# A four-part graph network on one core: batches from high destinations first, ten compare rows on ScalarE, the encoder's chunks shifted by two, and the first unit of a GRU step made in the sweep before it

## The reference

```
x = layernorm(x + gcn3(x))        # three convolutions h = segment_sum((h @ W)[src] * norm, dst) + b, then @ Wl + bl
x = layernorm(x + sage2(x))       # two layers h @ W_self + mean_agg(h) @ W_neigh + b
x = layernorm(x + ggnn(x))        # encoder, five GRU steps, decoder:
#   agg = segment_sum((h @ w)[src], dst); r, z = sigmoid(...); n = tanh(i_n + r * h_n); h = (1-z)*n + z*h
x = layernorm(x + gcn1(x))        # norm from counts, with self loops
```

## Time and profile before

| | |
|---|---|
| Median of 3 runs | 5464.75 us (5461.94 to 5466.56) |
| The profiled execution | 5469.89 us, span 5467.3 us |
| Mean granted TensorE clock | 0.91 |
| TensorE busy | 4736.8 us, 87% |
| TensorE weight loads | 2547.9 us, 47% |
| GpSimd busy | 2486.2 us, 45% |
| VectorE busy | 1805.1 us, 33% |
| ScalarE busy | 1189.7 us, 22% |

### The profile page before, as it was taken

The page is one execution under the profiler, slowest core; times in us unless marked ns, Lnnn a source line. Parts: engine busy times, 40 slices in busy tenths (PEclk is TensorE's granted clock), DMA queues, the critical chain, the costliest instruction groups (busy, mean ns, idle before and its releaser), DMA issues. The chain is left out here.

```text
span 5467.3 us, 77806 instructions
## 1 busy us (share of the span) xinstructions
PE 4736.8 (87%) x25659; PEld 2547.9 (47%) x25659; DVE 1805.1 (33%) x3217; ACT 1189.7 (22%) x2478; POOL 2486.2 (45%) x1708
## 2 busy tenths in 40 slices
PE   3544544499899999999998999899999999999999
PEld 3544444444344444444453544444444444444444
DVE  9999999910001000110050201302113031130642
ACT  4555555411011111111120101202112021120320
POOL 5888888888888888888888000000000000000000
PEclk7555555599999999999999999999999999999999
DMA  9999993399899999999988786595775857768477
GB/s 355 367 365 338 340 312 54 31 319 283 255 287 296 279 299 288 295 277 299 281 237 234 249 280 223 167 299 183 250 248 183 299 177 256 239 192 298 143 229 249
DMA packets 717675, 1402.14 MB, mean 256 GB/s; under 512 B 268948, under 2 KB 356840, under 8 KB 692456
## 3 DMA queue, kind: packets, MB, share of 16 engines
q1 hardware_dynamic: 477388, 1342.89, 73.5%
q0 software_dynamic: 225792, 0.70, 7.9%
q10 hardware_dynamic: 14364, 56.99, 2.8%
HBM read 1160.09 MB, written 240.26 MB: 256 GB/s over the span
## 5 line engine op out<-in xcount | busy, mean ns | idle before, releaser
L877 PE MATMUL psum<-arena 128*128 128x512 f16 (+3 forms) x14014 | 3665.3, 423 | 70.8 <-DMA arena<-C_adj 31.8
L877 PEld LDWEIGHTS psum<-arena 128*128 (+2 forms) x14014 | 1668.0, 123 | 2006.0 <-issue 924.8
L572 POOL DMA_INDIRECT W_adj<-arena x784 | 1214.0, 1548 | 278.9 <-issue 246.9
L572 POOL DMA_INDIRECT C_adj<-arena x784 | 1217.3, 1553 | 247.0 <-issue 247.0
L727 POOL TENSOR_TENSOR arena<-arena 128x512 f32 (+1 forms) x13 | 21.8, 1678 | 1716.1 <-DVE arena L1275 1716.1
L442 DVE TENSOR_SCALAR_CACHE_REDUCE arena<-arena 128x2048 bf16<-128x2048 f32 (+7 forms) x392 | 709.1, 1873 | 0.0
L520 PE MATMUL psum<-arena 128*128 (+1 forms) x6664 | 211.2, 167 | 561.9 <-DVE arena L467 335.9
L520 PEld LDWEIGHTS psum<-arena 128*128 128x128 bf16 x6664 | 207.0, 104 | 570.2 <-issue 516.7
L1471 DVE COPY arena<-psum 128x512 f32<-128x512 f32 (+1 forms) x39 | 23.2, 654 | 1139.7 <-PE psum L895 1139.7
L274 ACT ACTIVATE arena<-arena 128x1024 bf16<-128x1024 f32 (+7 forms) x392 | 298.4, 773 | 453.8 <-DVE arena L480 271.9
L1473 DVE TENSOR_SCALAR arena<-psum,arena 128x512 f32<-128x512 f32 x30 | 21.9, 748 | 1038.9 <-PE psum L877 1038.9
(11 more groups left out here) (238 smaller groups left out, 2575.0 us busy)
## 6 DMA issues: line engine op xcount, KB each, us to landing
arena<-C_adj SPq DMA_DIRECT2D x784, 384.0 KB, 3.8
arena<-W_adj SPq DMA_DIRECT2D x294, 768.0 KB, 4.3
arena<-C_adj SPq DMA_DIRECT2D x392, 512.0 KB, 4.5
arena<-W_adj SPq DMA_DIRECT2D x147, 1024.0 KB, 5.2
arena<-C_adj SPq DMA_DIRECT2D x392, 288.0 KB, 3.7
arena<-W_adj SPq DMA_DIRECT2D x147, 576.0 KB, 4.8
W_adj<-arena SPq DMA_DIRECT2D x12, 6400.0 KB
W_adj<-arena SPq DMA_DIRECT2D x12, 6144.0 KB
```

The source lines that it names most:

```text
L572: return pool.indirect_dma_start(table, bass.IndirectOffsetOnAxis(idx[:, t:t + 1], 0), values[:, of:of + 1], None, compute_op=ALU.add)
L877: ins = pe.matmul(psum[:, bank + b, 0:width], lhs, ring[:, slot, b * BANK:b * BANK + width], start=begin and part == 0, stop=False, skip_g ...
```

## The change

1. `ORDER` is reversed, so batches come from high destinations down. The padding edges move from the end of the last original batch to the end of batch 0 (the lowest destinations, now last) and get source NP - 1 and destination 0; their number is taken off one degree. The tables are zeroed from block 12 downwards, and `zones`, `limits` and `needed` are turned to match. The first product with each table (stages start and gcn 2) uses sweeps from the top, the last of one block.
2. `DVE_ROWS` goes from 8 to 6: ScalarE does rows 6 to 15. VectorE waits for the two added rows ahead of its first product with `near`.
3. In enc, the chunks of a unit are two earlier in number, and one is put ahead of the next unit's products. Three are left for after the loop instead of one.
4. In stages gru 0 to 3 and out, unit 0's products, gates and new state are made during the last sweep of the stage before, in laps 2 and 3 of it (`head` on ScalarE and VectorE, banks 0 to 3), and its transposes follow after lap 3 into bank 7. The stage then begins with `products(1, 1)` and chunk 0.

```diff
+ORDER = ORDER[::-1]
-DVE_ROWS = TB // 2
+DVE_ROWS = 6
+DOWNWARD = ((9, 4, 0), (5, 4, 4), (1, 4, 0), (0, 1, 4))
+ENC_LAG = 2
+HEAD_BANKS = (0, 1, 2, 3)
+HEAD_TURNED = 7
+HEAD_LAPS = 4
...
-            for z in range(BLOCKS):
+            for done, z in enumerate(reversed(range(BLOCKS))):
...
-            pool.memset(limits[:, k:k + 1], float((first + n) * BANK)).then_inc(s["ramps"], 1)
+            pool.memset(limits[:, k:k + 1], float(first * BANK)).then_inc(s["ramps"], 1)
...
-        dve.tensor_scalar(needed, limits, nearest[:, 0:1], order[:, 0:1], ALU.is_gt, ALU.mult) \
+        dve.tensor_scalar(needed, limits, farthest[:, 0:1], order[:, 0:1], ALU.is_le, ALU.mult) \
...
-        dve.tensor_scalar(zones, zones, 16.0, 16.0, ALU.mult, ALU.add).then_inc(s["zones_set"], 1)
+        dve.tensor_scalar(zones, zones, -16.0, 16.0 * BLOCKS, ALU.mult, ALU.add).then_inc(s["zones_set"], 1)
...
+            dve.wait_ge(s["late_rows"], b * (TB - DVE_ROWS) + half - DVE_ROWS)
...
+        link(dve.tensor_scalar(deg[0:1, 1, 0:1], deg[0:1, 1, 0:1], -float(PAD_EDGES), None, ALU.add))
...
+def sweeps_of(name, arg):
+    return DOWNWARD if (name, arg) in (("start", None), ("gcn", 2)) else SWEEPS
...
             def encoded(j, q):
-                spell((j - 1) * UC)
                 seconds(j, q)
-                spell((j - 1) * UC + 1)
+                spell((j - 1) * UC - ENC_LAG + 1)
...
                 for j in range(UNITS):
+                    spell((j - 1) * UC - ENC_LAG)
                     if j + 1 < UNITS:
                         products(j + 1, (j + 1) % 2)
                     encoded(j, j % 2)
-                for c in range((UNITS - 1) * UC, CHUNKS):
+                for c in range((UNITS - 1) * UC - ENC_LAG, CHUNKS):
...
-                products(0, 0)
+                if not headed(stages, k):
+                    products(0, 0)
                 products(1, 1)
-                seconds(0, 0)
+                if not headed(stages, k):
+                    seconds(0, 0)
...
+                    if sweep == SPLIT and headed(stages, k + 1):
+                        for lap in range(HEAD_LAPS):
+                            if lap == 2:
+                                pe.wait_ge(s["sum_dve"], base.sum_dve)
+                                pe.wait_ge(s["sum_act"], base.sum_act)
+                                pe.wait_ge(s["kept"], kept_before(stages, k + 1))
+                                gate_products(0, HEAD_BANKS)
+                                last_gate(0, HEAD_BANKS[3])
+                            for u in range(LAP):
+                                chunk(lap * LAP + (u + 1), u, sweep, 16 * lap + 16 * (laps + 1))
+                        if stages[k + 1][0] == "gru":
+                            pe.wait_ge(s["unit_set"], units_before(stages, k + 1) + 1)
+                            for c in range(UC):
+                                ins = pe.transpose(psum[:, HEAD_TURNED, c * P:(c + 1) * P], unit_out[:, 0, c, :], ident)
+                            ins.then_inc(s["seconds"], 1)
```

More of the change, by code:

```diff
@@ L84, in walk, with walk_on @@
     with eng.Fori(0, (UNITS - 1) // 2) as i:
+        for q in (1, 0):
+            j = 2 * i + (2 - q)
+            lead(j, q)
+            after(2 * i + (1 - q), 1 - q)
+            main(j, q)
+    after(UNITS - 1, 0)
+def walk_on(eng, lead, main, after):
+    lead(1, 1)
+    main(1, 1)
+    lead(2, 0)
+    after(1, 1)
+    main(2, 0)
+    with eng.Fori(1, (UNITS - 1) // 2) as i:
         for q in (1, 0):
@@ L594, in last_layer, with headed, bases_before, kept_before @@
     return last
+def sweeps_of(name, arg):
+    return DOWNWARD if (name, arg) in (("start", None), ("gcn", 2)) else SWEEPS
+def headed(stages, k):
+    return k < len(stages) and stages[k][0] in ("gru", "out")
+def bases_before(stages, k):
+    base = Bases()
+    for stage in stages[:k]:
+        base.advance(*stage)
+    return base
+def kept_before(stages, k):
+    return 1 + UNITS * sum(((n, a) in (("gcn", 2), ("enc", 1)) or n == "gru") for n, a, _ in stages[:k])
 def blocks_of(sweep):
@@ L745, in sync @@
             wide_before = wide
-            for sweep, (first, n, _) in enumerate(SWEEPS):
+            for sweep, (first, n, _) in enumerate(sweeps_of(name, arg)):
                 c0 = first * BANK
@@ L1116, in after, with head @@
                                        ACT.Copy).then_inc(s["chunk_set"], 1)
+            def head(ahead, following):
+                for gate, (to, bias) in enumerate(((gate_r, br), (gate_z, bz))):
+                    act.wait_ge(s["probs_in"], 2 * ahead.gates + gate + 1)
+                    act.activation(to, psum[:, HEAD_BANKS[gate], :], ACT.Sigmoid, bias=bias).then_inc(s["gates_set"], 1)
+                act.wait_ge(s["products_read"], ahead.read + 1)
+                act.activation(new_n, pre_n, ACT.Tanh, bias=col["bi2"]).then_inc(s["new_set"], 1)
+                if following == "gru":
+                    act.wait_ge(s["unit_set"], units_before(stages, k + 1) + 1)
+                    act.activation(unit(h_fm, 0), unit_out[:, 0].rearrange("p c f -> p (c f)"), ACT.Copy) \
+                        .then_inc(s["kept"], 1)
             def last_unit(j):
@@ L1191, in scalar @@
                             last_unit(j)
+                    if sweep == SPLIT and headed(stages, k + 1):
+                        head(bases_before(stages, k + 1), stages[k + 1][0])
                     if not wide:
@@ L1257, in vector @@
             base_units, base_new = units_before(stages, k), new_before(stages, k)
[L1258 to L1259 removed]
+            kept = kept_before(stages, k)
             dve.wait_ge(s["kept"], kept)
@@ L1416, in vector @@
             else:
-                with step.loop(0, (UNITS - 1) // 2, 2 * per) as i:
+                if headed(stages, k):
+                    main(1, 1)
+                    after(1, 1)
+                    main(2, 0)
+                with step.loop(1 if headed(stages, k) else 0, (UNITS - 1) // 2, 2 * per) as i:
                     for q in (1, 0):
```

92 lines of the change are left out of this document (65 added, 27 removed).

## The result

In 14 runs of each, the changed kernel takes 5452.16 us in the median (5448.01 to 5456.56), the kernel before 5462.24 (5458.25 to 5467.33): a ratio of 0.9981, 95% interval 0.9973 to 0.9989. The forecast was 5428, with a range up to 5450. So the gain is 10 us instead of 37, and the time lies just above the range. The profiled execution has a span of 5450.1 us against 5467.3, 17.2 less; the one of before was 7.6 us above its own median.

A forecast was written before the change was run, and what follows sets the result against it. GpSimd's adds, then the first C product's last sweep and TensorE's remaining products were taken to bound the kernel. Parts 1 to 4 summed 0 + 1 - 17 - 21 = -37 us, giving 5428 us against the median, range 5400 to 5450.

The forecast's parts named there:

- What bounds the kernel: GpSimd's 1568 adds to 3009.7 us, then the first C product's last sweep, then TensorE's seven more C products.
- Rival B: In GpSimd's adds: VectorE's relief quickens them, so the build's 125 us reach the end; 5308 us, chance 0.03.
- Part 1: Ten rows on ScalarE: the build ends near 975 us, but the 125 us saved are hidden by GpSimd; gain 0.
- the cover: TensorE's slack before C_adj is complete, which hides build time: 39 us even without any gain in the build.
- Part 2: High destinations first: last C sweep gains 18.4 us, GpSimd ends 19 later (14 to 29); net 1 us later.
- rival A: At the short last sweep and zeroing: loads keep up with TensorE and zeroing isn't waited for; 5404 us, chance 0.14.
- rival D: At GpSimd's start: zeroing holds it, each block beyond the count costing 40.7 us; 5469 or 5510 us, chance 0.07.
- Part 3: Encoder chunks shifted by two: 10 of 11 stands of 1.68 us and two at the tail covered; gain 17 us.
- Part 4: First unit made in the preceding sweep: idle time at five stage starts goes; gain 21 us (16 to 26).
- The sum: Parts 1 to 4 together: 0 + 1 - 17 - 21 = -37 us, giving 5428 us against the median.
- rival C: In encoder and heads: ScalarE and VectorE bind, so a covered stand reappears one wait later; 5460 us, chance 0.10.

The follow-up runs named there:

- e3: The changed kernel with eight rows on VectorE again instead of six (without Part 1): 5431.55 us, 0.9937 of the kernel before.
- e6: The changed kernel with loads of the second W sweep and the second W product's first sweep held to three in flight: 5434.02 us, 0.9948 of before.
- e1: The changed kernel with its first four batches ordered so that no neighbours share a destination: 5434.77 us, 0.9940 of the kernel before.
- e7: e1 with sweeps of 4, 4, 3 and 2 blocks in each table's first product, so two in the last: 5434.77 us in one run.

## Why the prediction was wrong, point by point

- **What bounds the kernel** was right. The rest behind the last add depends only on the code that stands there: it is 2397.9 to 2400.8 us in the seven kernels with the short last sweep and Parts 3 and 4, whatever GpSimd does before, and the build's 119.5 us (125 predicted) vanish in TensorE's waits. Rival B, adds quickened by VectorE's relief, is out: 1550 and 1553 ns.
- **Part 1, "price 0": this step failed.** Two things were missed. First, the work hidden by the cover isn't without effect: when TensorE starts the W product 119.5 us earlier, the turn from its first sweep to the second, with its burst of loads, comes just ahead of a stand of GpSimd, and the turn to the second product falls on a landing that GpSimd waits for. This costs 8.2 + (14.8 - 3.6) = 19 us on the path (the 3.6 from e3). e3 shows the whole sum, 17.7 by the last add. For the landing e6 shows the cause by a second way. For the stand the cause is a coincidence in time, seen long in after and e1 and short in e6 and e7; what is held up in it stays open. I asked only whether TensorE would still arrive in time, and not whom its transfers would meet. Second, the row used for GpSimd's idle time ends with 7.4 us of waiting for VectorE's first indices. A faster compare shortens that, when the zeroing doesn't cover it.
- **Part 2.** The sweep was sized rightly: from the last add to the end of the product 37.6 us instead of 56.3, a gain of 18.8 against 18.4. Loads at 0.65 us set it, against 0.60 predicted (e7's sweep, without a stand, bears it out), and rival A is out. The zeroing was 18.1, within 12 to 19. The two landings were sized at 4, bounds 2 to 10, from a row (1.5 us) that had no loads around it. They took 6.3 and 14.8 in after and 6.6 and 3.6 in e3, so even without the burst, with 10.2 together, they lie just over the bound. Against a predicted delay of 19, measured is 41.1: in the words of the prediction, this is a GpSimd that "has no slack", held by something other than rival D's zeroing.
- **Part 3** was right: from the stage's start to the first eviction 162.86 us instead of 182.63, 19.8 against 17; units follow each other at 11.47 us against 11.6 predicted.
- **Part 4** was right: the stretches from the enc stage's last sweep through out are 21.7 us shorter, against 21.
- **The sum** by the trace: 41.1 - 18.8 + 1.9 (sage) - 19.8 - 21.7 = -17.3, which is the change of the span. Predicted was 19 - 18 - 17 - 21 = -37. Of the difference of 20, 22 stand at GpSimd: 3 at the second batch, 17 at the two landings (21.1 against 4), 8 at the stand, less 6 from the shorter stands. The rest of the way to the measured 10 us is that the profiled execution of before was a long one.
- **The chances**: rival C's idea, a stand that comes back one wait later, didn't happen. No rival had the mechanism that decided. Each of the parts was weighed alone, and the loss was one that only two of them make together.

## What to carry to other kernels

Work off the critical path still moves transfers. When such work gets faster, ask which transfers now start when, and whether an engine on the path waits for a landing, or stands for a reason that the trace doesn't name, at that moment. Price a wait for a landing from a row with the same traffic around it, not from a quiet one. When a reordering pays at one end and costs at the other, see whether each table (or phase) can have its own order: here that turned -10 us into -69. And sum the parts in pairs where they touch the same engine.

## What the runs showed of the hardware

- GpSimd stood 3.6 to 6.6 us for the landing of a batch's small scatter-adds in e3 and e6, and in after for the first table; it stood 14.8 us in a stretch at 399 GB/s behind eight loads of 1024 KB issued in 20 us.
- GpSimd's issue of indirect DMAs has a stand about every seven batches (112 adds), mostly 1 to 7 us. The one near 1140 us took 11.85 and 12.45 us at 398 and 400 GB/s, and 3.7 and 3.9 us at 214 and 241 GB/s; but one in before took 3.69 us at 384, and one in e7, near 2187, took 7.41 at 402.
- SyncE issues a load of 128 x 512 float16 about every 0.65 us in its loop, with the ring free (57 in 37.30 us); TensorE needs one only each 0.91 us for two blocks.
- Zeroing W_adj took 0.0886 us a column with pieces of 256 columns, 0.0822 with 512.
